# Spreading tiny count products behind the sums of a group, and emptying a counted block first, in the first phase of a fused graph network

## The reference, cut to what matters

```
x = _layernorm(x + _L0_gnn_ref(x, ..., src, dst, edge_type_8))      # two relational layers
x = _layernorm(x + _L1_gnn_ref(x, src, dst))                        # sum of neighbours
x = _layernorm(x + _L2_gnn_ref(x, edge_index, ...))                 # attention
x = _layernorm(x + _L3_gnn_ref(x, edge_attr_128, src, dst))         # sum of neighbours and edge attributes

# inside _L0_gnn_ref, for each of its two layers l:
msg = T[etype, src] * norm
agg = jax.ops.segment_sum(msg, dst, num_segments=N)
h = relu(batch_norm(agg + h @ self_loop[l]))
```

## Time and profile before

| what | us |
|---|---|
| median of 3 runs | 6646.34 (6645.26 to 6676.93) |
| the profiled execution's own time | 6596.08 |
| its span in the trace | 6594.3 |
| stretch of the phase in which POOL gathers (165 to 3640) | 3475 |
| granted clock of TensorE, mean | 0.827 |

### The profile page before, as it was taken

How to read it: one execution, slowest core, us unless ns; L and a number is a source line. 1 busy time by engine, 2 the same in 40 slices (tenths; PEclk the granted TensorE clock), 3 DMA queues, 4 the chain that set the end, 5 groups by cost and what they waited for, 6 DMA issues and landing times. The chain is left out here.

```text
span 6594.3 us, 158005 instructions
## 1 busy us (share of the span) xinstructions
PE 4572.3 (69%) x54120; PEld 3419.2 (52%) x54121; DVE 3830.4 (58%) x8449; ACT 2466.9 (37%) x3932; POOL 2432.9 (37%) x2046
## 2 busy tenths in 40 slices
PE   5465556556666666666666499999989566666879
PEld 2244444444444444444444366666655366666868
DVE  4155555555555555555555566666640699999942
ACT  2122323223323323323323366666620355555700
POOL 0444444444454444454444000000000077776700
PEclk9777777777777777787777699999999778888889
DMA  5444444444444444444444422222259333344378
GB/s 199 139 126 138 139 137 142 136 136 138 139 138 138 140 135 137 141 139 137 139 137 142 146 77 80 77 79 77 78 189 299 111 142 145 148 156 150 113 234 282
DMA packets 678649, 935.70 MB, mean 142 GB/s; under 512 B 150867, under 2 KB 573374, under 8 KB 672542
## 3 DMA queue, kind: packets, MB, share of 16 engines
q1 hardware_dynamic: 469222, 545.66, 26.1%
q10 hardware_dynamic: 152888, 273.31, 11.3%
q0 software_dynamic: 56448, 115.72, 7.0%
HBM read 653.23 MB, written 281.17 MB: 142 GB/s over the span
## 5 line engine op out<-in xcount | busy, mean ns | idle before, releaser
L643 POOL DMA_INDIRECT f_rows<-table,f_recs x1715 | 1654.0, 964 | 1902.3 <-DMA f_recs<-edge_records 1187.8
L756 PE MATMUL f_acc<-f_rows,f_hot 128*128 128x264 f32 x3430 | 1214.2, 521 | 366.7 <-issue 285.1
L756 PEld LDWEIGHTS f_acc<-f_rows,f_hot 128*128 128x128 f32 x3430 | 868.8, 263 | 573.2 <-issue 348.4
L2067 PE MATMUL a_psum<-state_and_spare,a_weights 128*128 (+1 forms) x4802 | 664.3, 309 | 303.6 <-DVE a_weights L2200 168.9
L2017 POOL TENSOR_TENSOR a_weights<-a_powers,a_counts 128x896 f32<-128x896 f16 x245 | 713.6, 2917 | 315.9 <-ACT a_powers L2107 285.6
L2067 PEld LDWEIGHTS a_psum<-state_and_spare,a_weights 128*128 128x128 f32 x4802 | 653.7, 225 | 317.2 <-issue 215.0
L1224 ACT ACTIVATE g_grow<-g_gps 128x512 f16<-128x512 f32 x1225 | 667.1, 595 | 343.1 <-PE g_gps L1161 343.1
L816 ACT ACTIVATE f_counts_by_destination<-f_pm 128x896 f16<-128x896 f16 x343 | 314.5, 917 | 1011.5 <-PE f_pm L723 836.3
L705 PE MATMUL f_cnt<-f_dhot,state_and_spare 32*128 32x32 f16 x9604 | 239.2, 182 | 614.2 <-issue 614.1
L1181 PE MATMUL g_zps<-g_ohot,g_grow 32*128 32x256 f16 x19992 | 655.7, 269 | 0.0
L1263 DVE TENSOR_SCALAR g_ohot<-count,slot_target 128x256 f16<-128x256 f16 x2499 | 537.2, 282 | 152.4 <-PE g_zps L1181 147.0
(11 more groups left out here) (280 smaller groups left out, 6006.6 us busy)
## 6 DMA issues: line engine op xcount, KB each, us to landing
f_rows<-in_edge_attr SPq DMA_DIRECT2D x343, 320.0 KB
g_srow<-slot_sources SPq DMA_DIRECT2D x245, 320.0 KB
counts_by_destination_f<-f_counts_by_destination ACTq DMA_DIRECT2D x343, 224.0 KB
no_edge_penalty<-f_pen ACTq DMA_DIRECT2D x343, 224.0 KB
s_ring<-counts_by_destination_f SPq DMA_DIRECT2D x98, 784.0 KB
a_pen<-no_edge_penalty SPq DMA_DIRECT2D x49, 1568.0 KB, 10.0
a_counts<-counts_by_source_f SPq DMA_DIRECT2D x49, 1568.0 KB, 6.8
e_ring<-counts_by_source_f SPq DMA_DIRECT2D x343, 224.0 KB, 3.7
```

The costliest lines, as they stand in the source:

```text
L643: e.indirect_dma_start(out=rows[:, j, 0:D], out_offset=None, in_=k.table_d[0], in_offset=bass.IndirectOffsetOnAxis(ap=recs[:, j, 4:5].bitc ...
L756: m = e.matmul(acc[:, 0:GW], hot[:, j, :], rows[:, j, :], start=j == 0, stop=j == SLOTS - 1)
L2067: m = e.matmul(psum[:, 4 + i // 3, i % 3 * (D + 4):i % 3 * (D + 4) + D + 1], weights[:, j, i * P:(i + 1) * P], k.msg[:, bass.ds(hb * SEG + ...
```

## The change

`count` is cut in two: `begin_count` holds the waits and the 8 products of 512 columns, and `count_cells` the tiny products of a range of column tiles. In groups 2 to 5 the five sums are no longer issued together. Behind the first sum comes `begin_count` with its two waits, and behind each of the last four a quarter of the tiny products: 16 for a full block. The increment of `ring` stays on the last sum, which now stands behind 56 of the block's 72 products. On ACT, a counted block is emptied and stored ahead of the turned piece that it used to follow. The tail behind the loop and the first tile keep the old order. No instruction is added or taken away.

```diff
-            def count(t, b):
+            def begin_count(t, b):
 
                 lo, n = BLOCKS[b]
                 e.wait_ge(shot_made, t * (len(BLOCKS) + 1) + (b + 2))
@@
-                for j in range(n):
+
+            def count_cells(b, first_cell, end_cell):
+
+                lo, n = BLOCKS[b]
+                for j in range(first_cell, end_cell):
                     for u in range(QUARTERS):
                         q = slice(u * QW, (u + 1) * QW)
                         m = e.matmul(cnt[:, u, j * QW:(j + 1) * QW], shot[q, b % 2, j, :], dhot[q, lo + j, :],
                                      start=False, stop=j == n - 1)
-                m.then_inc(counted, 1)
+                return m
...
-                    for j in range(g * PER, (g + 1) * PER):
+                    b = g - 2
+                    between = 0 <= b < len(BLOCKS) and not first
+                    for i in range(PER):
+                        j = g * PER + i
                         m = e.matmul(acc[:, 0:GW], hot[:, j, :], rows[:, j, :], start=j == 0, stop=j == SLOTS - 1)
-                    m.then_inc(ring, 1)
+                        if i == PER - 1:
+                            m.then_inc(ring, 1)
+                        if between and i == 0:
+                            begin_count(t - 1, b)
+                        n = BLOCKS[b][1] if between and i else 0
+                        part = range((i - 1) * n // (PER - 1), i * n // (PER - 1))
+                        if len(part):
+                            c = count_cells(b, part.start, part.stop)
+                            if part.stop == n:
+                                c.then_inc(counted, 1)
@@
-                        if 2 <= g < 2 + len(BLOCKS):
-                            count(t - 1, g - 2)
@@ ScalarE
                 for b, (lo, n) in enumerate(BLOCKS):
-                    if b:
-                        move_turned(t, b - 1)
                     e.wait_ge(counted, t * len(BLOCKS) + (b + 3))
...
                                 mine[:, lo:lo + n, :].rearrange("p j d -> p (j d)")).then_inc(stored, 16)
+                    if b:
+                        move_turned(t, b - 1)
```

More of the change, by code:

```diff
@@ L706, in count @@
                                      start=False, stop=j == n - 1)
-                m.then_inc(counted, 1)
+                return m
+            def count(t, b):
+                begin_count(t, b)
+                count_cells(b, 0, BLOCKS[b][1]).then_inc(counted, 1)
             def turn_counts(t, g, final=False):
```

## The result

The changed kernel took 6710.33 us (6706.79 to 6717.18, 6 runs) against 6669.52 us (6645.26 to 6684.43, 6 runs) for the kernel before: ratio 1.0073, interval 1.0046 to 1.0100. I forecast 6610 us, a small gain. It is a small loss.

The account below looks back on a forecast made before the run. It took PE's slow instruction supply during POOL's gathers as the bound. Group steps summed to -1.2 us a tile, -56 us; allowing for lost short tiles it took -36, giving 6610 us, range 6440 to 6720.

Parts of the forecast that it names:

- That POOL's gathers slow PE's supply: Tiny products: while POOL gathers, PE gets instructions only slowly once a stock is used up; gaps of 614.1 us.
- Group 2, -2.8: Block 0: the stop comes earlier, but holding `ring` ends POOL's gathers sooner, so group 3 begins 2.8 us earlier.
- Group 3, +5.5: Block 1: one sum covers the wait for ACT to empty block 0, so PE stands near 4.9 us; +5.5 us.
- Group 4, -4.1: Block 2: the ACT exchange removes old waits and the stop is 4.8 us against 8.0; -4.1 us.
- Group 5 and on, -0.5: Block 3: shorter wait for block 2's emptying, one more pair of switches, sums partly at upper clock; -0.5 us.
- The next tile's place step, +0.7: Placing L688: POOL gathers groups 4 to 6 in one run, and the placing falls behind it 0.7 us later.
- The short tiles of before: Some old tiles are short, one 61.4 us; if such are lost, the gain is 70.4 - 70.3, nearly 0.
- The first rival: Stops in groups 2 and 4 do not follow POOL and keep their lengths: +7 us a tile, 6975; chance 0.07.
- The second: Group 3 meets the slow supply too, a third stop in block 1: +1.3 us a tile, 6705; chance 0.23.
- The third: The tile rhythm shifts for good, settling at 66 us: -4.6 us a tile, 6430; chance 0.25.
- The switches, up to 3.3 us a tile: Changes between sums and quarter-row tiny products in blocks 0 to 3: 13 more pairs at 0.25 us; bounds 0 and 3.3.

Follow-up runs that it names:

- lumped: `block0_first` with all 72 products of a block behind the first sum instead of quarters behind the last four: 5639.66 us, ratio 0.9990.
- block0_first: The changed kernel, with ACT emptying block 0 ahead of the self terms and piece 6, except in the last tile: 5651.14 us, ratio 1.0013.

## Why the prediction was wrong

Here the condition is that with stops, unless said.

*That POOL's gathers slow PE's supply.* Held as far as the first two traces go: over the 46 tiles of each trace all of the idle time inside the tiny products (608 and 253 us) lies within a run of gathers or at most 3 us behind its end, stretches that make up 77 and 78% of the time, and the shortened runs shortened the stops. It was never tried by an edit, since the stops did not come back, and the later traces show that gathers are not enough for them. Their cause stays open.

*Group 2, -2.8.* Measured -3.0 in the mean (-3.5 in the median): right, by the stop that I described. (A sum at 2.4 GHz takes 0.49 us by the rows, 2.44 over five, and not 0.44; nothing hangs on it.)

*Group 3, +5.5.* Measured +6.1 (+7.1). The wait is 4.70 us, I said 4.9. The size was off by the clock: I had half of the sums behind the wait at the lower level, and the trace shows all four, and the ranking behind them too (2.05 us where the nine products take 1.15 at 2.4 GHz).

*Group 4, -4.1.* Measured -4.3 (-5.7). *Group 5 and on, -0.5.* Measured -1.7 (-1.0).

*The next tile's place step, +0.7.* **This step failed**: +5.3 (+4.8). I had seen that POOL would gather groups 4 to 6 in one run of 15 into the next tile, and that the placing would meet its end. I then let it end with the run. In the trace the run ends 8.1 us into the tile instead of 6.7, full pace is back 2.5 us later instead of 2.0, and the placing's rest and the ranking run at the lower clock (the nine ranking products take 2.05 us against 1.15). The placing went from 3.1 to 7.0 us. Of the 7.0 us of gaps a tile that blocks 0 and 2 gave up, 3.4 came back here, and the products themselves take 1.9 us longer. With 0.7 in its place the sum would have been -2.2 a tile; with the measured one it is +2.4.

*The short tiles of before.* Their loss was in the sum: no tile of the changed kernel is under 69 us, where four of before took 61 to 62. The forecast of 36 us less used it with part of its weight. I then put that difference on a median of 6646; with six runs it is 6670. In the medians the change costs 41 us or 0.9 a tile, against the traces' 2.4, so a part of the +2.4 belongs to this one execution of the kernel before. The placing stands out all the same: its step is +4.8 in the median tile.

*The first rival* (stops keep their lengths) did not happen. *The second*, slower through a third stop in group 3 at 1.3 us a tile and 6705 us, has the right time by luck: no stop in group 3, but a longer one in the placing. *The third*, a faster rhythm, did not happen.

*The switches, up to 3.3 us a tile.* Their price of 0.25 us a pair holds in PE's own time (0.24 in group 3, 0.18 in group 4 without stops). What they cost the tile is open, since `lumped` changed the clock as well; those behind the head of DVE's chain cost nothing there. I added them where I should have asked whether PE was on the path.

What the forecast did not have at all is the chain on DVE. It is why the wait in group 3 and the slow clock behind it reach the tile in full without stops, 8.4 us of it: they delay block 1 and the ranking behind it, and the 20.6 us from there on stay as they are. In the first two traces that stretch is 29.1 us before and 22.9 after, so the head came 8.6 us later and the stops given up behind it paid back 6.2; within 2.3 us of the chain, little more was left to gain there.

## What to carry to other kernels

Before an engine's idle time is priced, follow who consumes the result that is late: here 20 us of another engine hung on the end of one block or ranking, and what PE saved behind that point did not shorten the tile. When products are spread between sums, their waits move with them; see what used to cover the wait. And when a stall has no releaser in the profile, take a second profile elsewhere before building on it: here the same kernel ran in 6670 and in 5645 us.

## What the runs showed of the hardware that was not expected

On the same program, the time of the kernel before was 6645 to 6684 us in the first six runs and 5629 to 5659 in five later groups. In the slower condition PE took 10.2 us in the median tile from block 0's first tiny product to its last, with idle gaps of up to 2.6 us that name no releaser, while POOL issued indirect DMAs or at most 3 us behind; in the other the 64 products take 0.85 us beside the same DMAs. The packets of POOL's queue took 7.0% of the 16 DMA engines' time in the span of 6594.3 us and 8.4% in that of 5635.4, about the same time in all. The cause is not known. A wait of 4.7 us on PE brought the clock to 1.2 GHz for the following 5.6 us of sums, four sums with their batches at 1.41 us instead of 0.85. Changing from full-array to quarter-row products and back lost 0.25 us in start times, and 0.18 to 0.24 us of PE's busy time in the means of `block0_first` and `lumped`.
